# Loading and splitting layer-1 key and value weights earlier, and a new order of the first tiles

## The reference

```python
x = _layernorm(x + _L0_ffn_ref(x, ...))    # routed experts: each row is x + sum over its 2 experts
x = _layernorm(x + _L1_attn_ref(x, ...))

def _L1_attn_ref(x, ...):                  # 16 heads of 32
    Q, K, V = heads(x @ qw + qb), heads(x @ kw + kb), heads(x @ vw + vb)
    feature_map = lambda t: jax.nn.elu(t @ fw1 + fb1) @ fw2 + fb2     # 32 -> 64 -> 64
    Qm, Km = feature_map(Q), feature_map(K)
    KV, Z = einsum('bhsf,bhsd->bhfd', Km, V), Km.sum(axis=2)
    num, den = einsum('bhsf,bhfd->bhsd', Qm, KV), einsum('bhsf,bhf->bhs', Qm, Z)
    return (num / maximum(den, 1e-06)).reshape(b, s, D) @ ow + ob
```

## Time and profile before

| what | us |
|---|---|
| median of 3 runs | 1608.56 |
| lowest and highest run | 1604.08, 1609.27 |
| the profiled execution's own time | 1606.87 |
| its span in the trace | 1605.1 |
| TensorE matmul busy in it | 1358.1 (85%) |
| VectorE, ScalarE, GpSimd busy | 1074.1, 728.6, 750.3 |

### The profile page before, as it was taken

One profiled execution on the slowest core, in us unless ns is written; L12 is line 12 of the kernel. 1 busy time (PEld: TensorE's weight loads), 2 busy tenths in 40 slices (PEclk: granted clock), 3 DMA queues, 4 the chain that ended last, 5 costly groups with the idle time before them and its releaser, 6 DMA issues. The chain is left out here.

```text
span 1605.1 us, 21477 instructions
## 1 busy us (share of the span) xinstructions
PE 1358.1 (85%) x7252; PEld 1118.4 (70%) x7253; DVE 1074.1 (67%) x1792; ACT 728.6 (45%) x1157; POOL 750.3 (47%) x656
## 2 busy tenths in 40 slices
PE   6999869999699999925999689996698899999960
PEld 5787647766477777725999688995566777777740
DVE  5688747232388888846885556764393688888857
ACT  4121132000188888822554354441422388888850
POOL 1455510000488887632664324331056467777744
PEclk9899979999799999967999899997799799999995
DMA  4000040000456566533110100000512899999958
GB/s 165 1 1 27 27 132 2 1 0 0 161 190 222 170 208 226 171 120 95 52 53 2 31 3 1 28 27 27 194 40 103 319 335 341 342 346 346 345 134 314
DMA packets 81807, 212.67 MB, mean 132 GB/s; under 512 B 20425, under 2 KB 23497, under 8 KB 79291
## 3 DMA queue, kind: packets, MB, share of 16 engines
q1 hardware_dynamic: 50075, 133.14, 22.7%
q0 software_dynamic: 31120, 77.38, 17.0%
q10 hardware_dynamic: 528, 1.05, 0.2%
HBM read 208.75 MB, written 46.79 MB: 159 GB/s over the span
## 5 line engine op out<-in xcount | busy, mean ns | idle before, releaser
L66 PE MATMUL bank<-e_w_hi,e_xt_hi 128*96 128x384 f32 (+1 forms) x444 | 169.3, 381 | 3.4 <-DVE e_w_lo L2551 3.4
L68 PE MATMUL bank<-e_w_hi,e_xt_lo 128*96 128x384 f32 (+1 forms) x444 | 161.8, 364 | 0.0
L67 PE MATMUL bank<-e_w_lo,e_xt_hi 128*96 128x384 f32 (+1 forms) x444 | 161.3, 363 | 0.0
L1051 POOL DMA_INDIRECT e_w_raw<-in_w_gate_up,r_load_of x47 | 53.4, 1135 | 218.5 <-issue 218.5
L2441 POOL DMA_INDIRECT sums<-e_y,r_target_of x64 | 110.2, 1722 | 70.1 <-DMA sums<-e_y,r_target_of 44.0
L1176 DVE TENSOR_TENSOR e_w_lo<-e_w_raw,e_w_hi 128x2048 fp32r<-128x2048 f32 x47 | 107.7, 2292 | 33.8 <-ACT e_w_hi L1135 33.8
L2551 DVE TENSOR_TENSOR e_w_lo<-r_w_early,e_w_hi 128x1536 fp32r<-128x1536 f32 x48 | 84.9, 1768 | 24.4 <-ACT e_w_hi L2515 24.4
L1043 POOL DMA_INDIRECT e_xg<-rows,r_token_of x47 | 93.2, 1983 | 14.3 <-issue 14.3
L231 POOL TENSOR_TENSOR a_read<-a_read_n 128x256 f32<-128x256 f32 x64 | 50.2, 785 | 103.1 <-DVE a_read_n L452 103.1
L1675 POOL TENSOR_TENSOR q_g_lo<-q_gf,q_g_hi 128x512 fp32r<-128x512 f32 x32 | 41.5, 1298 | 111.9 <-ACT q_g_hi L1789 111.9
L1135 ACT ACTIVATE e_w_hi<-e_w_raw 128x2048 fp32r<-128x2048 f32 x47 | 89.8, 1910 | 0.0
(11 more groups left out here) (461 smaller groups left out, 4361.7 us busy)
## 6 DMA issues: line engine op xcount, KB each, us to landing
r_w_early<-in_w_gate_up SPq DMA_DIRECT2D x48, 768.0 KB, 16.6
r_w_early<-in_w_down SPq DMA_DIRECT2D x24, 768.0 KB, 13.2
results<-e_y SPq DMA_DIRECT2D x47, 256.0 KB, 5.0
rows<-resid SPq DMA_DIRECT2D x8, 1024.0 KB, 4.3
r_w_first<-in_w_gate_up SPq DMA_DIRECT2D x8, 768.0 KB, 16.4
e_w_raw<-in_w_down SPq DMA_DIRECT2D x8, 768.0 KB, 13.5
e_w_raw<-in_w_gate_up SPq DMA_DIRECT2D x8, 768.0 KB, 16.1
resid<-in_x SPq DMA_DIRECT2D x4, 1024.0 KB, 12.5
```

Source lines behind the costliest of these rows:

```text
L66: pe.matmul(out, a_hi, b_hi, start=start, stop=False)
L67: pe.matmul(out, a_hi, b_lo, start=False, stop=False)
L68: return pe.matmul(out, a_lo, b_hi, start=False, stop=stop)
L1051: pool.indirect_dma_start(w1_raw[p][:, :], None, io["w_gate_up0"], bass.IndirectOffsetOnAxis(k.load_of[:, c:c + 1], 0), bounds_check=E0 * ...
```

## The change

- The raw key and value weights get buffers of their own (`k.kw_raw`, `k.vw_raw`), allocated around `experts0_routed`, as do the raw feature weights and bias. SP issues these seven loads ahead of the store of group `NG0 - 6`, and at the end of that block waits for them.
- In `attention1_keys`, ScalarE rounds both weights first thing, and VectorE first zeroes and splits the feature weights (zeroing was GpSimd's) and then both weights, ahead of `combine(0)`. The bias work stands behind `combine(1)`.
- The shared schedule starts in a new order (below). `combine(i)` of tiles 2 and 3 stands around the first turns, `keys(0)` and `keys(1)` ahead of the turns of pair 1 and of everything for pair 2.
- SP loads the query weights at the start of the block. The loads of small weights (L1322 to L1326) wait for GpSimd's zeroing as before.
- GpSimd's larger zeroings move from behind the first gathers into `combine(4)`, behind gather 5, as `zeros()`; `fw2_t`'s waits for the feature and bias work (`s_fw`). First users wait for the new counts.
- `g_hi` and `g_lo` are one buffer shared by the keys and queries parts, and several small buffers are allocated in another order, so that they take the memory of the early raw buffers.

```diff
             def _(sp):
...
                 def store(h, p):
+                    if isinstance(h, int) and U * h + p == NG0 - 6:
+                        for name, raw in (("kw", k.kw_raw), ("vw", k.vw_raw)):
+                            sp.dma_start(raw[:, :, :], io[name].rearrange("(b p) n -> p b n", p=P)).then_inc(s_kv, 16)
+                        for n in range(4):
+                            sp.dma_start(k.fw1_raw[n * DH1:(n + 1) * DH1, :], io["fw1"]).then_inc(s_kv, 16)
+                        sp.dma_start(k.fb1_raw[:, :], io["fb1"].partition_broadcast(P)).then_inc(s_kv, 16)
                     sp.wait_ge(s_ysb, U * h + p + 1)
...
+                sp.wait_ge(s_kv, 16 * 7)
...
-            for c in range(3):
-                combine(2 * c)
-                combine(2 * c + 1)
-                rstd(c)
-                normalise(c)
-                if c < 2:
-                    turn(2 * c)
-                    turn(2 * c + 1)
+            combine(0)
+            combine(1)
+            rstd(0)
+            normalise(0)
+            combine(2)
+            turn(0)
+            turn(1)
+            combine(3)
+            rstd(1)
             keys(0)
+            normalise(1)
             keys(1)
+            turn(2)
+            turn(3)
+            combine(4)
+            combine(5)
+            rstd(2)
+            normalise(2)
             for i in range(NT):
...
             def _(sp):
-                sp.dma_start(raw[:, :, :], io["kw"].rearrange("(b p) n -> p b n", p=P)).then_inc(s_kw, 16)
-                for h in range(4):
-                    sp.dma_start(fw1_raw[h * DH1:(h + 1) * DH1, :], io["fw1"]).then_inc(s_fw, 16)
                 sp.dma_start(kb[:, :], io["kb_t"]).then_inc(s_kb, 16)
                 sp.dma_start(vb[:, :], io["vb"].partition_broadcast(P)).then_inc(s_vb, 16)
-                sp.dma_start(fb1[:, :], io["fb1"].partition_broadcast(P)).then_inc(s_fb, 16)
-                sp.wait_ge(s_wlo, 1)
-                sp.dma_start(raw[:, :, :], io["vw"].rearrange("(b p) n -> p b n", p=P)).then_inc(s_vw, 16)
-
-                sp.wait_ge(s_zero, 13)
+                sp.dma_start(raw[:, :, :], io["qw"].rearrange("(b p) n -> p b n", p=P)).then_inc(w["s_qw"], 16)
+                sp.wait_ge(s_zero, 11)
...
-                sp.wait_ge(s_wlo, 3)
-                sp.dma_start(raw[:, :, :], io["qw"].rearrange("(b p) n -> p b n", p=P)).then_inc(w["s_qw"], 16)
...
             @block.scalar
+                act.activation(kw_hi[:, :, :], k.kw_raw[:, :, :], ACT.Copy).then_inc(s_whi, 1)
+                act.activation(vw_hi[:, :, :], k.vw_raw[:, :, :], ACT.Copy).then_inc(s_whi, 1)
+                act.wait_ge(s_kb, 16)
...
             @block.vector
+                vec.memset(fw1_hi[:, :].bitcast(F32), 0.0).then_inc(s_fwz, 1)
+                vec.memset(fw1_lo[:, :].bitcast(F32), 0.0).then_inc(s_fwz, 1)
+                vec.wait_ge(s_fwz, 2)
...
+                    vec.tensor_copy(fw1_hi[r, c], fw1_raw[r, :]).then_inc(s_c, 1)
...
+                    last = vec.tensor_tensor(fw1_lo[r, c], fw1_raw[r, :], fw1_hi[r, c], ALU.subtract)
+                last.then_inc(s_fw, 1)
+                for n, (raw_, hi, lo) in enumerate(((k.kw_raw, kw_hi, kw_lo), (k.vw_raw, vw_hi, vw_lo))):
+                    vec.wait_ge(s_whi, n + 1)
                     vec.tensor_tensor(lo[:, :, :], raw_[:, :, :], hi[:, :, :], ALU.subtract).then_inc(s_wlo, 1)
...
                 def tile(i):
...
+                    else:
+                        vec.wait_ge(s_zero, 7)
+                        vec.wait_ge(s_vb, 16)
...
                     ln_stats(k, vec, i, s_stat, i)
+                    if i == 1:
+                        feature_bias()
```

## The result

The changed kernel took 1599.46 us in the median (1595.75 to 1602.85, 7 runs) against 1604.19 us (1603.53 to 1609.27, 7 runs) for the kernel before on the same chips. The ratio is 0.996 with a 95% interval of 0.9944 to 0.9975: 6.4 us faster by the ratio (4.0 to 9.0), 4.7 by the medians. The forecast was 1600.9, 7.7 us faster than the 1608.56 that the kernel before had in its first three runs.

What follows compares the result with a forecast made beforehand. TensorE was taken to bound the keys loop from 792 us, with idle waits before it. The first value read 7.7 us earlier, other terms 0, gave 1606.87 - 7.7 = 1599.2, or 1600.9 against the 1608.56 median; range 1596.5 to 1606.5.

Steps and rivals of the forecast that it cites:

- Raw loads cost nothing: Last layer-0 blocks: seven more load issues on SP cost 0; without cover up to 10.4 us would be exposed.
- D: Rival: the raw loads disturb layer 0, two megabytes fully exposed, 10.4 us, giving 1611.3; chance 0.04.
- GpSimd is held up, tile 1 lands 1.2 later: Block start: VectorE's subtractions delay tile 1's gathers, between 0 and 2.5 us; 1.2 taken, landing at 709.3.
- keys(0): First key products on TensorE: run from 720.1 to 724.4, 11.8 us earlier than before.
- keys(1): Second key products on TensorE: cost between 2.7 and 5.1 us by clock; 4.0 taken, ending at 730.2.
- turn(4): Third pair's first turn on TensorE: idle from about 734 to 742 ahead of it, giving back some 4 us.
- keys(2): Key products behind the third pair's first turn: 10 matmuls at 0.21 and 14 at 0.11, ending at 746.9.
- the mark: First read of value products (L1550), end of the starting chain: from 757.89 to about 750.2, 7.7 us gained.
- Behind the mark nothing changes: After the first value read: both kernels queue the same work in the same order, nothing changes per tile.
- Rival A: Block start free and clock high: tile 1 lands at 708.1, gain 10.2 us, 1598.4; chance 0.15.
- B: Rival: late gathers and a low TensorE clock in the block's start, gain only 2.9 us, 1605.7; chance 0.15.
- C: Rival: VectorE becomes the bound, third pair normalised at 742.1 against 740.5, 1.6 us slower, 1610.2; chance 0.06.

Runs made afterwards that it cites:

- x3: The changed kernel with the 1 MB query-weight load moved behind GpSimd's zeroing; ran once, keys and queries blocks 427.4 us.
- x8: The changed kernel with the query-weight load as the first of the block's three SP issues; ran once, keys and queries blocks 427.4 us.
- x1: The changed kernel with the old order of first tiles, early raw loads and splits kept; ratio to the kernel before 0.9972.
- x9: x1 with VectorE's value-weight subtraction moved back behind keys(1); ran once, keys and queries blocks 426.7 us.
- x6: x5 with tile 4's combination moved between keys(0) and keys(1), tile 5's between the turns of pair 1; median 1595.07 us, ratio to the kernel before 0.9937.
- x7: x6 with the query weights loaded behind GpSimd's zeroing; median 1595.06 us, ratio to the kernel before 0.9932.
- x5: The changed kernel with keys(2) moved from behind turn(4) to behind combine(5); median 1598.88 us, ratio to the kernel before 0.995.
- x4: The changed kernel with VectorE's two 2.28 us subtractions moved behind the combinations of tiles 2 and 3; ran once, keys and queries blocks 428.5 us.

## Why the prediction was right, and where it was off

The time came out 1.4 us from the forecast partly by luck. The forecast starts from 1608.56, the median of three runs, two of which were the slowest of the seven; over all seven it is 1604.19. The same 7.7 us taken off that would have given 1596.5, 3.0 below what was measured. The gain itself was forecast too large: 7.7 against 4.7 by the medians and 6.4 by the ratio, though the interval (4.0 to 9.0) holds it.

The steps, in its own order, all counted from the block's start:

- *Raw loads cost nothing.* Right: the routed block took 276.03 us against 276.64. D is out, and so is a late block start.
- *The splits just fit.* Right: VectorE was done at 7.2, as worked out.
- *GpSimd is held up, tile 1 lands 1.2 later.* The mechanism was right, 2.59 and 1.90 us. The size was not: by the view of DMA issues tile 1's second gather landed at 11.0 against 10.6 before, and in x3 and x8, with the same slow issues, at 10.5 and 10.4. I looked for the price at the wrong tile. The load that I called the same as the one before is issued 0.86 later, between tile 0's gathers, and with that tile 0 is combined 2.6 us later than before. Two errors met: tile 1's combination followed tile 0's at 12.16, where I had 11.9. That this step came out nearly right is luck.
- *Bias work under the wait for rstd.* Right: 1.7 us, normalising at 16.2 against my 16.0.
- *keys(0)* at 22.9, my walk 22.7.
- *keys(1)* took 4.65 us, from 721.67 to the read at 726.32; I took 4.0 between 2.7 and 5.1. More of it ran at the low clock than I assumed.
- *turn(4)* behind 8.3 us of idle time, at 45.3; I had 44.7 and about 8. The giving back was foreseen.
- *keys(2)* ended at 50.8 instead of 49.5. I took 3.3 us at the low clock from the earlier trace rows; here the low clock lasted from 737.73 to about 742.05, 4.3 us. The mark is at 53.6 instead of 52.8: a gain of 6.8, forecast 7.7.
- *Behind the mark nothing changes.* This step failed. From the mark to the end of the block it took 157.5 us against 156.3, and the queries block 216.1 against 215.05, 2.3 us together: the larger part of what separates the 7.7 from the 4.6 of these blocks.

Where the 2.3 lie can be read from the table of windows. First the keys block behind the mark, the kernel before and the changed one; then the queries block of the kernel before, of the changed one and of x1:

```profile
757.89:914.18 156.29, 144.92 (x1048) 136.31 (x1047) 111.30 (x179) 76.92 (x150) 85.06 (x74) 0.96 0.10 29
746.06:903.54 157.48, 145.76 (x1048) 137.40 (x1046) 111.51 (x179) 76.83 (x150) 85.13 (x74) 0.95 0.10 28
914.18:1129.22 215.04, 187.63 (x1242) 172.57 (x1242) 129.85 (x242) 85.12 (x146) 69.33 (x66) 0.90 0.07 24
903.54:1119.65 216.11, 189.02 (x1242) 173.64 (x1242) 129.94 (x242) 85.11 (x146) 69.28 (x66) 0.89 0.07 24
905.70:1118.73 213.03, 186.03 (x1242) 170.98 (x1242) 129.66 (x242) 85.22 (x146) 69.46 (x66) 0.92 0.07 24
```

TensorE makes the same 1048 and 1242 matmuls in each. In the changed kernel it is busy 0.8 and 1.4 us longer with them, 2.2 together, at a lower granted clock; its idle time is 0.35 longer in the one block (1.91 us ahead of the first `sums` instead of 1.57) and 0.3 shorter in the other. So the 2.3 us are matmuls that ran at the low clock. One place of it is the last `sums` ahead of the queries block, the kernel before first, then the changed one:

```profile
902.40:907.40 5.00, 2.90 (x16) 2.79 (x16) 0.00 (x0) 0.20 (x1) 2.05 (x2) 0.79 0.00 0
```

```profile
892.45:897.45 5.00, 3.62 (x16) 3.49 (x16) 0.59 (x4) 0.00 (x0) 0.65 (x1) 0.50 0.00 0
```

Both follow a wait of 3.0 us for GpSimd, behind the same full work. The same 16 matmuls ran at clock 0.79 in the one and 0.50 in the other, and took 0.7 us more. Why the clock is low at other places in one kernel than in the other isn't shown: the waits lie shifted by some us, but no run shifts them alone. The size isn't small beside the differences between variants: x1 lost 2.7 us behind the mark and took 3.1 less than the changed kernel in the queries block, where the code is the same and TensorE was busy 3.0 less, at 0.92. That is why x1 and x9 read 0.4 to 0.5 better than the changed kernel in the sum of the blocks though their mark is 1.2 later.

Rival A didn't happen (tile 1 landed only 0.4 later than before, but tile 0 was late), B in part: a low clock for longer. C, VectorE as the bound, was wrong at the mark: the third pair was normalised 2.1 us later than before (44.2 against 42.1) and the mark came 6.8 earlier. It was half right ahead of it: x6 shows that the chain to turn(4) ran through VectorE's combinations.

## What to carry to other kernels

A wait names the last operation of a queue. Before crediting a move with that wait, take the operations ahead of it out one by one: here the value split was named, and what stood ahead of it in the queue was the price. And an early start (keys(0) 11.6 us earlier) is worth what the next item of the same in-order queue leaves of it; walking all the queues to one common mark found that some 4 us of it would be given back (4.8 were), and moving what blocked it, keys(2) and two combinations, won 5 us more at that mark.

## What the runs showed of the hardware

- Tile 0's second gather lands 3.9 to 4.1 us after its issue when no 1 MB load is beside it (x7, x3). With such a load issued 0.68 us ahead of the tile's first gather it lands after 5.7 (x8; 5.2 in the kernel before), with the load issued between the two gathers after 7.3 to 7.8 (x5, x6, the changed kernel), though the bytes are the same. The load itself landed later too: 8.4 us after its issue in the changed kernel, where it took 5.2 in the earlier trace rows.
- An indirect DMA's issue is held up beside a two-input VectorE operation between SBUF tensors (2.59 and 1.90 us against 0.95 in x4). The Trainium skill, "GPSIMD Engine Reference", section Key points, names contention between GpSimd and VectorE instructions with two SBUF inputs, and the runs agree; they add that the landing need not move, since the gather of x3 took 2.5 us from the end of its issue instead of 5.3 in the earlier trace rows.
- The low clock after an idle stretch lasted 3.3 us in the earlier trace rows and 4.3 us ahead of the changed kernel's mark; equal work behind equal waits ran at 0.79 in one kernel and at 0.50 in another. Over the queries block the same 1242 matmuls kept TensorE busy from 186.0 us (x1, clock 0.92) to 189.0 us (changed, 0.89) with the same idle time, 27.0 and 27.1.
